# Queries begun beside the last feed-forward steps, first scores and maxima moved under the queries, and inputs rounded a step sooner in the last stage

## The reference

```python
x = x + _L0_xattn_ref(_layernorm(x), ctx, Wq, bq, Wk, bk, Wv, bv)   # one head of 256
x = x + _L0_ffn_ref(_layernorm(x), ...)    # 3 blocks: linear, layernorm, gelu, linear, residual
x = x + _L1_xattn_ref(ctx, _layernorm(x), w_q, w_kv, w_out, b_out)  # 16 heads of 16
x = x + _L1_ffn_ref(_layernorm(x), norm1_w, w1, act_scale, act_bias, norm2_w, w2)
```

## Time and profile before

| what | us |
|---|---|
| median of three runs | 1267.38 |
| the profiled execution | 1262.24 |
| its span, first to last instruction | 1260.3 |
| PE busy | 1074.0 (85%) |
| DVE busy | 865.5 (69%) |
| ACT busy | 529.4 (42%) |
| POOL busy | 515.5 (41%) |

### The profile page before, as it was taken

How to read it: one execution, slowest core, us unless ns; L and a number is a source line. 1 busy time by engine, 2 the same in 40 slices (tenths; PEclk the granted TensorE clock), 3 DMA queues, 4 the chain that set the end, 5 groups by cost and what they waited for, 6 DMA issues and landing times.

```text
span 1260.3 us, 30832 instructions
## 1 busy us (share of the span) xinstructions
PE 1074.0 (85%) x9234; PEld 772.4 (61%) x9234; DVE 865.5 (69%) x2318; ACT 529.4 (42%) x953; POOL 515.5 (41%) x875
## 2 busy tenths in 40 slices
PE   2599999999999698989886489999999999766665
PEld 2477777777777556566654246666666666434443
DVE  2846665556656467676656488888888888388886
ACT  1332222222222211111113336666666666578886
POOL 0324444444444222221210224454555554566664
PEclk7699999999999899999898869999999999779898
DMA  9423333333332000000002797777878776630000
GB/s 214 127 71 88 90 91 91 91 91 91 91 89 81 18 1 0 0 0 0 1 1 50 155 159 149 157 160 159 156 163 161 159 157 139 206 118 25 25 25 29
DMA packets 121313, 116.06 MB, mean 92 GB/s; under 512 B 45075, under 2 KB 114230, under 8 KB 121270
## 3 DMA queue, kind: packets, MB, share of 16 engines
q1 hardware_dynamic: 121270, 115.55, 39.1%
HBM read 79.15 MB, written 36.00 MB: 91 GB/s over the span
## 4 chain that ended last, share of the span: by engine, by line
PE 48%; DVE 20%; issue 11%; ACT 9%; SPq 6%; DMA 3%; POOL 2%; DVEq 2%; POOLq 0%; ACTq 0%
PE bank L1495 25%; DVE nm L1281 7%; PE bank L1653 6%; PE bank L1589 3%; ACT v_all L1006 3%; ACT v_all L999 2%; ACT v_all L993 2%; DVE hT L1200 2%; PE bank L1765 2%; PE bank L1578 2%; DVE yn L1189 2%; PE bank L1735 1%; PE bank L1751 1%; POOL rs L706 1%; PE bank L1828 1%
## 5 line engine op out<-in xcount | busy, mean ns | idle before, releaser
L1281 DVE TENSOR_REDUCE nm<-bank 112x1 f32<-112x375 f32 x512 | 247.3, 537 | 14.9 <-PE bank L1735 14.2
L954 ACT ACTIVATE pT<-bank 125x448 f32<-125x448 f32 x384 | 185.0, 543 | 54.6 <-PE bank L1751 53.8
L1735 PE MATMUL bank<-ks,qs 96*128 96x375 bf16 x512 | 166.8, 338 | 24.2 <-DMA qs<-q_parts_dram 19.4
L1751 PE MATMUL bank<-qs,ks 128*128 128x112 bf16 x1536 | 138.0, 213 | 0.6 <-DMA qs<-mrow 0.6
L1751 PEld LDWEIGHTS bank<-qs,ks 128*128 128x128 bf16 x1536 | 112.2, 99 | 21.7 <-issue 1.0
L1765 PE MATMUL bank<-pT,vaug 125*32 125x112 f32 x3072 | 100.1, 263 | 0.0
L905 ACT ACTIVATE yT<-bank,bcol,gcol 128x448 f32<-128x448 f32 x48 | 32.2, 721 | 159.9 <-PE bank L1635 159.9
L1653 PE MATMUL bank<-wffT,hT 128*112 128x256 f32 x384 | 99.1, 391 | 0.0
L1495 PE MATMUL bank<-wv1T,ctxT 128*125 128x256 f32 x384 | 88.0, 379 | 0.0
L1495 PE MATMUL bank<-ctxT,wk1T 128*128 128x375 f32 x256 | 86.0, 478 | 0.0
L1765 PEld LDWEIGHTS bank<-pT,vaug 125*32 125x32 f32 x3072 | 69.2, 109 | 24.0 <-issue 15.9
(11 more groups left out here) (204 smaller groups left out, 2288.7 us busy)
## 6 DMA issues: line engine op xcount, KB each, us to landing
k_parts_dram<-kp SPq DMA_DIRECT2D x192, 93.8 KB, 3.5
ks<-k_parts_dram SPq DMA_DIRECT2D x64, 281.2 KB, 4.2
cnat<-in_ctx_dram SPq DMA_DIRECT2D x32, 375.0 KB
ks<-k_parts_dram SPq DMA_DIRECT2D x64, 187.5 KB, 3.9
ks<-k_parts_dram SPq DMA_DIRECT2D x64, 93.8 KB, 3.4
q_parts_dram<-qp SPq DMA_DIRECT2D x48, 112.0 KB, 2.2
qs<-q_parts_dram SPq DMA_DIRECT2D x64, 84.0 KB, 4.0
x_stream<-in_x_dram SPq DMA_DIRECT2D x4, 896.0 KB, 14.9
```

Of the source, the lines that this page charges most:

```text
L954: act.activation(pT[:, u % 6, :], B3[u % 3][0:TP], ACT.Exp).then_inc(probs_made, 1)
L1281: dve.tensor_reduce(nm[:, h:h + 1], A3[h % 3][0:L], AX_X, ALU.max, negate=True).then_inc(head_max_taken, 1)
L1735: mm(A3[h % 3], qs[par][0:KS, h * L:h * L + P], ks[par][0:KS, h * T:(h + 1) * T], start=True, stop=True).then_inc(max_scores_made, 1)
L1751: last = mm(B3[c][:, j * L:(j + 1) * L], ks[par][:, h * T + c * TP:h * T + c * TP + P], qs[par][:, h * L:(h + 1) * L], start=True, stop=True)
```

## The change

Five things are edited.

1. In the last turn of stage 2, DVE norms the rows of query groups 0 and 1 between its old steps, and PE turns group 0 there. All turned query rows now go to one PSUM tile YT[0], so each `rows_turn` also waits for ACT's copy of the one before. The loop over query groups is written out.
2. SP loads the keys of batch 0 before the first query store, and the queries of batch 0 behind the stores of groups 0 and 1.
3. The 16 score products and maxima of batch 0 are issued inside query steps 4 to 7, 3, 3, 5 and 5 heads (`FIRST`). They use two banks in turn instead of three, so head h waits until the maximum of head h-2 is taken. POOL's fills for batch 0 and the laying out of values come before the end of the stage.
4. Batch 1's first ten maxima move from ahead of batch 0's step into it, two heads at a time from the fourth unit on; `turn_m(1)` moves behind the scores of batch 0. On SP the maxima rows of batch 0 go between the two halves of batch 1's load.
5. In stage 4 DVE rounds the input of tile i+3 at the end of step i, instead of tile i+2 near its start, and ACT does `xq_out` before `hq_out`.

```diff
+        FIRST = [()] * (NG - 4) + [(0, 1, 2), (3, 4, 5), (6, 7, 8, 9, 10), (11, 12, 13, 14, 15)]
@@ SP
+            for s in range(2):
+                sp.wait_ge(x_after_ffn1[s], NG // 2)
+            for half in range(2):
+                load_keys(0, 0, half)
+            for s in range(2):
+                store_q(0, s)
+            sp.wait_ge(q_stored[0], 96)
+            for half in range(2):
+                load_queries(0, 0, half)
+            with sp.Fori(1, NG // 2) as i:
+                for s in range(2):
+                    store_q(i, s)
...
-            sp.wait_ge(q_stored[0], 96)
-            for half in range(2):
-                load_half(0, 0, half)
             for s in range(2):
                 sp.wait_ge(q_stored[s], 96 * (NG // 2))
+            load_half(1, 1, 0)
+            rows_m(0, 0)
+            load_half(1, 1, 1)
             everywhere_late(n1_bc[:, :], L1_ffn_norm1_w, D)
-            for half in range(2):
-                load_half(1, 1, half)
-            rows_m(0, 0)
@@ ACT, stage 4
             def step4(i, par, n):
+                if not isinstance(i, int) or i < NT - 2:
+                    xq_out(i + 2, par)
                 if not isinstance(i, int) or i >= 2:
                     hq_out(i - 2)
-                if not isinstance(i, int) or i < NT - 2:
-                    xq_out(i + 2, par)
@@ DVE, end of stage 2
                         if more:
                             norm_rows(i + 1, 1)
+                        else:
+                            normed(0, 0)
...
+                if not more:
+                    normed(1, 1)
+                    x3(i, 1)
                 keep(i, 0)
@@ DVE, queries
+            def query_step(e, s):
+                if e < NG - 2:
                     dve.wait_ge(q_rows_turned, e + 1)
                     normed(e + 2, s)
                 q_rest(e, s)
                 q_three(e, s)
+                for h in FIRST[e]:
+                    maxima(0, h)
@@ DVE, stage 4
-                if not isinstance(i, int) or i < NT - 2:
-                    round_x(i + 2, par)
...
                     inverse_x(i + 3, 1 - par)
+                    round_x(i + 3, 1 - par)
@@ PE, queries
+            def rows_turn(e, s):
+                pe.wait_ge(q_rows_normed, e + 1)
+                if e >= 1:
+                    pe.wait_ge(q_features_ready, e)
...
             def scores_for_max(b, par, n, h):
+                first = isinstance(b, int) and b == 0
...
+                if first and h >= 2:
+                    pe.wait_ge(head_max_taken, h - 1)
...
+            def query_step(e, s):
+                if e < NG - 1:
+                    rows_turn(e + 1, 1 - s)
+                query(e, s)
+                for h in FIRST[e]:
+                    scores_for_max(0, 0, 0, h)
@@ PE, stage 3
+                at_once = 1
+                if isinstance(b, int) and b == 0:
+                    heads = [(1, 1, 0, h) for h in range(AHEAD)] + heads
+                    at_once = 2
...
-                        if heads:
-                            scores_for_max(*heads.pop(0))
                         u = TC * g + c
+                        for _ in range(at_once if at_once == 1 or u >= TC else 0):
+                            if heads:
+                                scores_for_max(*heads.pop(0))
```

More of the change, by code:

```diff
@@ L486, in _, with store_q, load_keys @@
             stage_end(sp, "sp", 2)
[L489 to L503, removed]
+            def store_q(i, s):
+                sp.wait_ge(q_rest_part3_made, 4 * i + 2 * s + 2)
+                for part in range(3):
+                    for c in range(KC):
+                        sp.dma_start(
+                            qd[part, bass.ds((2 * i + s) * GB, GB), c].rearrange("b d h l -> (d h) b l"),
+                            qp[s][:, part, c].rearrange("p (b l) -> p b l", b=GB)).then_inc(q_stored[s], 16)
+            def load_keys(b, par, half):
                 heads = slice(half * H8, (half + 1) * H8)
@@ L511, in load_half, with load_queries @@
                                  one.unsqueeze(1).broadcast_to([DH, reps, H8 * T])).then_inc(half_in[half][par], 16)
-                    parts = reps
+                    at_row += n
+            def load_queries(b, par, half):
+                at_row = 0
+                for parts in (3, 2, 1):
+                    n = parts * DH
                     sp.dma_start(qs[par][at_row:at_row + n, half * H8 * L:(half + 1) * H8 * L],
@@ L515, in load_half @@
                     at_row += n
+            def load_half(b, par, half):
+                load_keys(b, par, half)
+                load_queries(b, par, half)
+            for s in range(2):
[10 more added lines that the diff above has]
+                    store_q(i, s)
+            sp.sem_inc(stage_done["sp"], 1)
+            for e in ENG:
+                if e != "sp":
+                    sp.wait_ge(stage_done[e], 3)
             def rows_m(b, par):
@@ L786, in _ @@
                 pool.wait_ge(ones_rows_made, b + 1)
+            for s in range(2):
+                pool.wait_ge(x_after_ffn1[s], NG // 2)
+            pads(0)
+            pool.wait_ge(q_rows_normed, 1)
+            for b in range(3):
                 pool.memset(vaug[b][:, :, H * VW:H * VW + VPAD], 0.0)
@@ L1325, in step3 @@
                 last = (par + 2) % 3
+                if isinstance(b, int) and b == 0:
+                    for h in range(H):
+                        maxima(1, h)
+                    parts_m(1)
+                    for h in range(AHEAD):
+                        maxima(2, h)
+                    return
                 for k in range(H):
@@ L1343, in step3 @@
                         parts_m(b + 1)
-            for h in range(H):
-                maxima(0, h)
             parts_m(0)
-            for h in range(AHEAD):
-                maxima(1, h)
             def max_x(i, par):
@@ L1456, in _ @@
             inverse_x(2, 0)
+            round_x(2, 0)
             late = CH * (NCH - 1) - 3
@@ L1813, in step3 @@
                             fin_project(b - 1)
-                        if (g, c) == (2, 2) and (not isinstance(b, int) or b < B - 1):
+                        if (g, c) == ((2, 2) if at_once == 1 else (4, 0)) and (not isinstance(b, int) or b < B - 1):
                             turn_m(b + 1)
-                if heads:
+                while heads:
                     scores_for_max(*heads.pop(0))
-            for h in range(H):
-                scores_for_max(0, 0, 0, h)
             turn_m(0)
-            for h in range(AHEAD):
-                scores_for_max(1, 1, 0, h)
             def in_turn(i, par):
```

97 lines of the change are left out of this document (46 added, 51 removed).

## The result

Four runs of the changed kernel gave 1275.45 to 1282.41 us, median 1280.91, beside 1267.32 for the kernel before (four runs). The ratio is 1.0103, 95% interval 1.0075 to 1.0132: slower by 13 us (9.5 to 16.7), above the top of the predicted range. The profiled execution of the changed kernel took 1280.63 us with a span of 1278.8. That is the median, while the profiled one of before was 5.1 under its median, so the spans (18.5 apart) overstate the change.

What follows compares the result with a forecast made beforehand. PE was taken to bound stage 3, ACT to be busiest in stage 4, and the two qp tiles to bound the queries. Entry +8.5 less stage 4's 6.0 gave +2.5 us, forecast 1270, whole range 1261 to 1277.

Steps and rivals of the forecast that it cites:

- stage 4: Stage 4: a step falls from 5.47 to 5.21 us with one wait of 0.43, 6 us gained in all.
- entry, until batch 1 begins: Queries and batch 0, up to batch 1's step in stage 3: batch 1 starts 8.5 us later.
- order of six DMAs in a load: SP's loads: the new order changes no count and costs nothing, bounded by 1 us each way.
- nothing gives it back later, since PE is the bound of every further step: Stage 3 from batch 1: the 8.5 us later start stays, with PE busy 322 of 345 us.
- The early start: Groups 0 and 1 normed inside stage 2: group 0's third part written at about 672.2, 9.0 us sooner.
- POOL's fills ... lie at 669 to 680 with POOL idle otherwise: Batch 0's fills on POOL during the queries: cost nothing, bounded with other edits by 0 and 1 us each way.
- SP's queue: Batch 0's query loads between stores of groups 1 and 2: group 2's store 2.7 us late, gain falls 9.0 to 6.3.
- The slower rival: PE's 2.2 us pause before group 2 lowers the clock, or it never recovers in the chain: +8, 1275; chance 0.2.
- The chain through the maxima: Query steps 4 to 7: products wait for DVE's maxima, 4.3 us pauses, slow restarts; queries end 14.8 us later.
- the rival by which it holds: Query chain: TensorE's clock stays up through 4.3 us pauses; sum -5, 1262.5; chance 0.13.
- Behind the queries: From last query to batch 1: shifted scores at 742.3, 2.2 later; batch 1's first maximum at 744.5, 8.0 late.
- The rival of 10 to 15: Stage 4: ACT is hardly kept waiting, the stage gives 10 to 15 us; 1263; chance 0.12.

Runs made afterwards that it cites:

- the interleaved kernel: The changed kernel with each half-load's six DMAs from batch 1 on issued again as keys, queries in alternation; 1.0022 of the kernel before.
- the late fills: As the changed kernel with alternating key and query loads, but GpSimd's pads behind group 4's norms and value tiles behind all norms; 1.0009 of the kernel before.
- the keys first: The kernel before with each half-load's three key DMAs issued ahead of its three query DMAs, nothing else; 1.0044, 5.6 us slower.

## Why the prediction was wrong

| part | forecast | measured |
|---|---|---|
| stage 4 | -6.0 (0 to -15) | -6.3 (-8.9 to -3.7), alone |
| entry, until batch 1 begins | +8.5 | +8.4 in the trace; +9 (6 to 12) as the interleaved kernel (+2.8) less stage 4 |
| order of six DMAs in a load | 0 (1 each way) | +10 (6 to 14) in the changed kernel, +5.6 (3.3 to 7.8) alone |
| sum | +2.5 | +13 (9.5 to 16.7) |

**The step that failed** is "the order of six DMAs within a load change no count", with its bound of 1 us, and under it "nothing gives it back later, since PE is the bound of every further step": a cost in SP's queue was put at next to nothing, and the queue was taken to have room. The first took the number of DMAs for the cost of issuing them; the last queries' DMA costs 0.16 more in the new order. The second read PE's 322 busy of 345 us as a bound and never put SP's own queue beside the step. That queue was there to be read: 12 loads, two stores and the rows of maxima, with SP waiting 1.0 us in 160. A cost of 0.3 us in a queue without slack, 28 times, is 8 to 10 us. No rival held this either. The slower one, 1275, put the loss in the entry and would have been right in sign only.

**The early start** came out: group 0's third part is written at 672.73+1.09-1.8 = 672.0 (672.2 forecast).

**"POOL's fills ... lie at 669 to 680 with POOL idle otherwise"** was true and beside the point, since DVE is not idle there. Group 1 was written at 680.2 instead of 677.4. PE waited 4.20 for these norms (678.92), the clock fell (0.62 granted from 680 to 684), the next product took 4.78 instead of 3.19, and group 2 was written at 687.1 instead of 681.9.

**SP's queue** hardly cost anything here: the store of group 2, to be 2.7 late behind the six query loads, was issued at 689.45, 0.5 behind the late group 2 itself. So group 4 at 697.2 instead of 694.3 is luck in part: one loss, not forecast, hid another, forecast. With the late fills the forecast one is seen, as group 4 is written at 693.62+1.09-0.44 = 694.3.

**The slower rival** asked whether PE's pause of 2.2 before group 2's turn lets the clock fall. It was 2.16, and from 668 to 676 the clock granted was 1.00: so the first 2.7 us of its price are out.

**The chain through the maxima** was right in place and size: waits of 4.92 and twice 4.57 (4.3 forecast) before heads 2, 5 and 8. Its three turns took 33.5 us instead of 35.2, as the restarts were cheaper. In step 5, turn and product take 0.66 and 1.09 more than at the full clock (turn to product 1.49 against 0.83, product 4.28 against 3.19): 1.75 and not 2.7; the last product took 2.41 more and not 2.0. Group 7 was written at 730.7 (729.5 forecast), so the late group 4 and the cheaper restarts nearly cancelled. Of the clock, the trace shows 0.71 granted from 700 to 740. It fell in pauses of 4.6 us, and the rival by which it holds is out. For a clock that holds through such pauses the prediction names "the first rival"; it means the second, the one at -5.

**Behind the queries**, less 1.8: shifted scores 742.4 (742.3 forecast), first maximum of batch 1 at 744.5 (744.5), batch 1 at 758.5 (758.6). Here too part of the agreement is luck. The rows of maxima were issued at 741.85-1.8 = 740.1 and not at 738.7, and the scores followed 2.4 behind and not 3.5. And ahead of batch 1 PE waited 2.10 for the queries of batch 2, a load in SP's queue that no term held, while turn to scores took 3.0 (757.30 to 760.29) and not 4.2.

**Stage 4**: 5.19 us a step with one wait of some 0.4 (5.21 and 0.43), 6.3 us in all (6). The rival of 10 to 15 is out.

Still open: why the changed kernel's last three batches are longer. The last three gaps of its rows of maxima are 11.11, 12.07 and 12.10 us, 35.3 together, and 12.07, 10.27 and 10.17 before, 32.5 together; of the 2.8 us some 0.9 are the order's. The kernel before with the keys first has 32.5 as well, and so has the interleaved one. Open too is what makes one gap of the changed kernel 12.46 and one of the interleaved 12.32.

## What to carry to other kernels

Before calling an engine the bound of a loop, add up each engine's instruction stream over one period, the DMA-issuing one included, which no busy share shows; where another stream is almost as long, easing the longest gains only the difference (0.13 us here), and loading it costs in full, times the number of periods. After moving work from one engine to another, look at who meets whom: here a small copy that began 0.04 us behind a neighbour's add took four times as long. Work put ahead of the next step of a pipeline must not wait for anything later than that step's own inputs: with two buffers, two heads a step fit and the third turned the pipeline into a chain. An idle engine was no free place here, since its neighbour was at work: GpSimd's fills made VectorE's norms 3.7 us longer.

## What the runs showed of the hardware

- The issue of one and the same DMA (16 rows of queries) took 0.37 us behind a DMA of keys over the same rows and 0.53 behind another DMA of queries; the other five of that half took 0.44 to 0.57 in either order.
- An increment of a semaphore shows as 17 ns on SP and took 58 ns of its queue. The Trainium skill, "DMA: Bandwidth & Descriptors", section "Issuing engines are not separate DMA queues", calls the sequencer's time to issue a DMA usually small beside the transfer. The trace agrees for each one: a load's issue takes 0.36 to 0.65 us, and it lands 3.3 to 4.2 us later (medians). But 15 issues in a row set the pace of stage 3.
- Four norms on VectorE took 5.12 us beside GpSimd's fills and copies and 1.38 without them. A copy of 112x2 on VectorE took 0.70 us begun 0.04 behind a GpSimd add on 112x256, and 0.16 begun 0.05 ahead of one.
- A DMA issued by ScalarE held it for 0.73 us, in which no activation ran.
